# An expert loop whose down products move one tile later, between the next tile's up products

## The chip, the core and the metric

The kernel runs on one core of a Trainium2 chip. A core has five engines that run side by side and meet only through semaphores: TensorE (PE: matrix products into the PSUM banks), VectorE (DVE), ScalarE (ACT), GpSimd (POOL) and SyncE (SP: it starts transfers). The metric is the device time of one execution in microseconds. The kernel before takes 276.58 us, the median of three runs from 275.57 to 281.17.

## The reference

The input x holds 32 sequences of 64 tokens of 128 numbers (2048 tokens); the layer has two parts.

```python
x = x + xattn(layernorm(x), ctx)          # projections, FFT over the sequence, Hamilton products
x = x + ffn(layernorm(x))

def ffn(x):                               # 8 experts, top 2
    gate_logits = x @ gate_w + gate_b
    weights, indices = top_k(gate_logits, 2); weights = softmax(weights)
    h = einsum('bsd,edh->ebsh', x, w1) + b1            # 128 -> 1024 for each expert
    xh, gh = split(h, 2)
    act = silu(gh) * xh                                # 512
    out_e = einsum('ebsf,efd->ebsd', act, w2) + b2     # 512 -> 128
    return sum over the two chosen experts of out_e * weight
```

The change is in the second part. Each of the 2048 tokens picks two experts, so 4096 rows are computed.

## The kernel before

**Routing.** The kernel computes only the chosen experts. After the first part it ranks the 4096 (token, choice) pairs by expert and cuts them into tiles of 256 rows that never mix experts; with these inputs there are 21 tiles, and `MAX_TILES` is 23. A grid of matrix products (L1101) turns the ranks into lists: for each tile, from which rows of `xn_rows` (normalised tokens, in memory) its inputs come and to which rows of `y_rows` its outputs go. They lie in `lists_all`. The names `bounds` and `ends` are the numbers of the tile at which each expert ends, values that are known only at run time.

**The expert loop.** Every engine has eight loops in a row, one for each expert e, whose count comes from `ends`; all engines go over the same tiles t.

- POOL gathers the 256 rows of a tile with two indirect DMAs (two halves of 128, L900) into one of two slots of `xg`, and scatters a tile's results with two more (L918) from one of two slots of `y_sb`. The row numbers of both are first copied to `lists_now` (L910). [...] Its order per tile is: copy the lists, gather tile t+3, wait for y of tile t, scatter tile t.
- DVE copies the gathered rows to `x_now` (L786, `move_x`), which frees the slot.
- PE transposes them (L1109, `turn_x`) into bank 4; ACT rounds that to `xT_hi` (L455) and DVE keeps the rest as `xT_lo` (L781).
- PE makes the up products in four chunks c of 128 hidden units (banks 0 to 3), each of two parts with three matmuls: w1_hi by xT_hi (L1133), w1_hi by xT_lo (L1134) and w1_lo by xT_hi (L1135). The last matmul of a chunk signals `up_done`.
- ACT applies silu to the gate part (L466, `silu_ready`), DVE multiplies with the other part (L808, `act_ready`).
- PE makes the down products of chunk c from `act` and w2 (L1145, banks 5 and 6), sums over the four chunks and signals `down_done` once per tile. DVE adds b2 into `y_sb` (L816, `y_ready`); that write waits until the scatter that last read the slot has landed.

The order on PE for a tile is: up 0 to 3, transposes of tile t+1, down 0 to 3. The order on DVE is: act 0 to 3, xT_lo of t+1, y, move_x of t+2. The order is written out by hand, and each engine works strictly in its own order. DVE also makes `w1_lo` of experts 4 to 7 (L558) after the loops of experts 0 to 3.

**After the loop** SP waits until all scatters have landed, reads `y_rows` back (L339), ACT and DVE combine the two choices, and the output is written (L342).

## Time and profile before

| | us |
|---|---|
| median of three runs (lowest, highest) | 276.58 (275.57, 281.17) |
| the profiled execution's own time | 275.91 |
| its span, first to last instruction | 274.1 |
| first up matmul of the expert loop to the last scatter's issue, in the span | 115.65 to 255.62 |

The profile shows one execution. Times in its rows are in microseconds from the span's start, and a group's row gives how often an instruction ran, its busy time, the mean of one in ns, and how long its engine stood idle just before it and for whom. A line number is one of the code above. In the trace, a matmul of 32-bit data is shown as two instructions where both operands are full float32 (L1145, L1109), and as one for the rounded kind (L1133 to L1135). `prod` is the name of both `act` and `silu`, and `spec` the one of both `xg` and `y_sb`, since they share memory with tiles of the first part. "issue" means that no recorded event released the instruction, and "remote" that the releaser is not among the recorded instructions.

### The profile page before, as it was taken

To read this page: it belongs to the slowest core of one execution; us is meant where nothing else is said; L and a number is where in the kernel's file an instruction comes from. 1 tells how busy PE (TensorE), PEld (TensorE's weight loads), DVE (VectorE), ACT (ScalarE), POOL (GpSimd) and SP (SyncE) were. 2 spreads that over 40 slices of the span, in tenths; PEclk is the share of its full clock that TensorE was granted. 3 is DMA by queue.
4 is the path that set the end of the run, shared out by engine and by line. 5 is a ranking of instruction groups with operands and counts; after the bars stand their busy time and mean duration, and the time that the engine had idled before them with its cause. 6 is when DMAs were issued, how large, how long until landed. Compare 5 with 4: busy or idle time off the path is not lost.

```text
span 274.1 us, 4826 instructions
## 1 busy us (share of the span) xinstructions
PE 206.2 (75%) x1454; PEld 186.3 (68%) x1454; DVE 161.8 (59%) x435; ACT 89.5 (33%) x211; POOL 135.6 (49%) x201
## 2 busy tenths in 40 slices
PE   8999998999596018679796996979799739887000
PEld 5898777889586006469695985969799729787000
DVE  4783896999957898335353742445466234354145
ACT  0473541112184073033233523242333124233033
POOL 0100444455900070746675886868688873856300
PEclk9977999999777555999999999799999977999755
DMA  7999200000026500110211011111111112222095
GB/s 213 305 339 316 62 0 0 2 0 0 11 85 182 200 0 0 38 42 29 45 31 48 29 46 40 48 29 43 42 41 38 49 41 30 48 29 48 22 282 174
DMA packets 17918, 20.76 MB, mean 76 GB/s; under 512 B 2736, under 2 KB 13520, under 8 KB 17872
## 3 DMA queue, kind: packets, MB, share of 16 engines
q1 hardware_dynamic: 13520, 14.08, 16.8%
q0 software_dynamic: 3008, 5.87, 8.8%
q10 hardware_dynamic: 1376, 0.64, 1.0%
q8 instruction: 7, 0.11, 0.2%
q14 instruction: 7, 0.06, 0.1%
HBM read 15.63 MB, written 4.95 MB: 75 GB/s over the span
## 4 chain that ended last, share of the span: by engine, by line
PE 39%; DVE 17%; issue 12%; POOL 11%; another core or an unknown queue 8%; DMA 5%; ACT 4%; DVEq 2%; POOLq 1%; SPq 1%; ACTq 0%
PE bank L1145 7%; POOL y_rows L918 5%; PE bank L954 4%; POOL spec L900 4%; PE bank L1135 4%; PE bank L1006 3%; PE bank L1007 3%; PE bank L1133 3%; PE bank L969 3%; PE bank L1134 3%; DVE prod L577 2%; PE bank L991 2%; DVE shared_a L754 2%; DMA spec<-xn_rows,lists_now 2%
## 5 line engine op out<-in xcount | busy, mean ns | idle before, releaser
L466 ACT ACTIVATE prod<-bank,b_col 128x256 f32<-128x256 f32 x84 | 38.5, 474 | 93.2 <-PE bank L1135 65.0
L1145 PE MATMUL bank<-w_sb,prod 128*128 128x128 f32 x336 | 51.9, 299 | 18.3 <-DVE prod L808 11.8
L1145 PEld LDWEIGHTS bank<-w_sb,prod 128*128 128x128 f32 x336 | 44.1, 203 | 25.2 <-DVE prod L808 16.9
L808 DVE SCALAR_TENSOR_TENSOR prod<-bank,b_col,prod 128x256 f32<-128x256 f32 x84 | 37.8, 480 | 34.3 <-ACT prod L466 17.4
L1133 PE MATMUL bank<-xT_hi,w_hi 128*128 128x256 f32 x168 | 49.3, 294 | 0.2 <-DVE xT_lo L781 0.2
L918 POOL DMA_INDIRECT y_rows<-spec,lists_now x42 | 42.6, 1015 | 10.0 <-issue 8.7
L1134 PE MATMUL bank<-xT_lo,w_hi 128*128 128x256 f32 x168 | 47.3, 281 | 0.0
L1135 PE MATMUL bank<-xT_hi,w_lo 128*128 128x256 f32 x168 | 47.2, 281 | 0.0
L900 POOL DMA_INDIRECT spec<-xn_rows,lists_now x40 | 42.1, 1052 | 9.2 <-issue 9.0
L1133 PEld LDWEIGHTS bank<-xT_hi,w_hi 128*128 128x128 f32 x168 | 31.8, 189 | 0.8 <-issue 0.6
L1134 PEld LDWEIGHTS bank<-xT_lo,w_hi 128*128 128x128 f32 x168 | 31.8, 189 | 0.0
L1135 PEld LDWEIGHTS bank<-xT_hi,w_lo 128*128 128x128 f32 x168 | 31.7, 189 | 0.0
L816 DVE TENSOR_TENSOR spec<-bank,b_sb 128x256 f32 x21 | 8.9, 425 | 38.4 <-PE bank L1145 19.7
L861 POOL TENSOR_TENSOR half<-prod 128x512 f32<-128x512 f32 x7 | 9.0, 1280 | 33.0 <-DVE prod L577 33.0
L895 POOL TENSOR_TENSOR taken<-const 1x1 f32<-1x1 f32 x41 | 8.6, 210 | 24.0 <-DVE spec L816 21.5
L884 POOL TENSOR_TENSOR shared_b<-basis,choice_b 128x832 bf16<-128x832 bf16 x2 | 4.8, 2416 | 22.4 <-DVE basis L749 22.4
L1006 PE MATMUL bank<-basis,spec 128*128 128x256 f32 x48 | 15.4, 404 | 0.6 <-ACT spec L390 0.6
L1007 PE MATMUL bank<-basis,spec 128*128 128x256 f32 x48 | 15.2, 399 | 0.0
L1109 PE MATMUL bank<-const,x_now 128*128 128x128 f32 x44 | 8.6, 278 | 6.5 <-DVE x_now L786 4.7
L577 DVE TENSOR_TENSOR prod<-q_basis,bank 128x512 f32<-128x512 f32 x16 | 10.2, 680 | 5.5 <-ACT q_basis L397 5.5
L954 PE MATMUL bank<-warm 128*128 128x256 bf16 x81 | 12.1, 323 | 1.2 <-DVE warm L514 1.2
L397 ACT ACTIVATE q_basis<-bank 128x256 f32<-128x256 f32 x8 | 3.1, 384 | 29.5 <-PE bank L1007 29.5
(173 smaller groups left out, 360.0 us busy)
## 6 DMA issues: line engine op xcount, KB each, us to landing
xq<-in_L_ffn_w SPq DMA_DIRECT2D x2, 1024.0 KB, 6.3
xq<-y_rows SPq DMA_DIRECT2D x8, 256.0 KB, 4.9
xq<-in_x SPq DMA_DIRECT2D x2, 512.0 KB, 6.2
x_sb<-in_L_ffn_w SPq DMA_DIRECT2D x1, 1024.0 KB, 12.1
w_spare<-in_L_ffn_w SPq DMA_DIRECT2D x1, 1024.0 KB, 12.6
xn_rows<-xq SPq DMA_DIRECT2D x4, 256.0 KB, 2.4
out<-ctx_sb SPq DMA_DIRECT2D x4, 256.0 KB, 2.4
const<-const_table SPq DMA_DIRECT2D x1, 690.5 KB, 9.0
```

Of the source, the lines that this page charges most:

```text
L466: nc.scalar.activation(silu[:, c, :], bank[:, c, XT:2 * XT], ACT.Silu, bias=b1_col[:, e * 2 * FC + FC + c:e * 2 * FC + FC + c + 1]).then_i ...
L577: last = tt(o, l, r, ALU.mult)
L808: stt(act[:, c, :], bank[:, c, 0:XT], b1_col[:, e * 2 * FC + c:e * 2 * FC + c + 1], silu[:, c, :], ALU.add, ALU.mult).then_inc(act_ready, 1)
L900: nc.gpsimd.indirect_dma_start(out=xg[:, par, h, :], out_offset=None, in_=xn_dram, in_offset=bass.IndirectOffsetOnAxis(ap=offsets[:, h:h + ...
L918: nc.gpsimd.indirect_dma_start(out=y_dram, out_offset=bass.IndirectOffsetOnAxis(ap=lists_now[:, par, 1, h:h + 1], axis=0), in_=y_sb[:, par ...
L954: mm(bank[:, 0, 0:256], warm[:, 0:P], warm[:], start=True, stop=True)
L1006: mm(dst, src[:, 0], basis[:, i, 0, :], start=False, stop=False, skip_group_check=True)
L1007: last = mm(dst, src[:, 1], basis[:, i, 1, :], start=False, stop=True, skip_group_check=True)
L1133: mm(dst, w1_hi[:, e, cols], xT_hi[:], start=True, stop=False)
L1134: mm(dst, w1_hi[:, e, cols], xT_lo[:], start=False, stop=False)
L1135: last = mm(dst, w1_lo[:, e, cols], xT_hi[:], start=False, stop=True)
L1145: last = mm(bank[:, 5 + h, 0:D], act[:, c, h * P:(h + 1) * P], w2_sb[:, e * FC + c, :], start=(c == 0), stop=(c == FC - 1))
```

## The change

1. **Down products one tile later.** In step t, PE does up 0, up 1 of tile t; down 0, down 1 of tile t-1; the transposes of tile t+1; up 2, up 3 of tile t; down 2, down 3 of tile t-1. After the last loop come the down products of the last tile. Step 0 makes down products of a tile that doesn't exist, and nothing scatters their result. Since tile t-1 can be of another expert, PE works out which w2 to take (`of`) in registers, and DVE which b2.
2. **Two slots** for `xT_hi` and `xT_lo`, since the transposes now come in the middle of the up products that read the other slot.
3. **Signals.** `down_done` is given per chunk, and DVE's product of chunk c waits for it (`act` has one slot per chunk, so the old tile's down product must have read it). DVE's order is act 0, act 1, xT_lo, act 2, y of tile t-1, act 3, move_x, copy of the lists. ACT's order is silu 0, silu 1, xT_hi, silu 2, silu 3.
4. **POOL.** The copy of the lists moves to DVE. One wait, for `lists_taken`, begins a step of POOL; then come the scatter and the gather, in that order. Gathers run five tiles ahead of the scatter beside which they stand (three before), and five tiles are gathered ahead of the loop. Tiles past the last are no longer gathered.
5. The lists have room for 24 tiles rather than 26 (`NCOL` 48, not 52).

```diff
-AHEAD = 3
-NCOL = HALVES * (MAX_TILES + AHEAD)
+AHEAD = 5
+NCOL = HALVES * (MAX_TILES + 1)
...
-        xT_hi = sb("xT_hi", [P, XT], F32R)
-        xT_lo = sb("xT_lo", [P, XT], F32R)
+        xT_hi = sb("xT_hi", [P, 2, XT], F32R)
+        xT_lo = sb("xT_lo", [P, 2, XT], F32R)
...
@@ ScalarE, once per tile
-                    keep_xT_hi(t + 1)
+                        if c == 1:
+                            keep_xT_hi(t + 1)
...
@@ VectorE
+            def keep_act(t, e, c):
+
+                v.wait_ge(silu_ready, FC * t + c + 1)
+                v.wait_ge(down_done, FC * t + c + 1)
+                stt(act[:, c, :], bank[:, c, 0:XT], b1_col[:, e * 2 * FC + c:e * 2 * FC + c + 1],
+                    silu[:, c, :], ALU.add, ALU.mult).then_inc(act_ready, 1)
+
+            def keep_y(t, of):
+
+                v.wait_ge(down_done, FC * t + FC)
+                for h in range(HALVES):
+                    v.wait_ge(scattered[0][h], ((t + 1) // 2) * 16 + 16)
+                    v.wait_ge(scattered[1][h], (t // 2) * 16 + 16)
+                tt(y_sb[:, bass.ds((t + 1) % 2, 1)].rearrange("p o h d -> p (o h) d"), bank[:, 5:7, 0:D],
+                   b2_sb[:, bass.ds(of, 1), :].to_broadcast([P, HALVES, D]), ALU.add).then_inc(y_ready, 1)
+
+            def copy_lists(t):
+
+                cp(lists_now[:, bass.ds((t + 1) % 2, 1)].rearrange("p o k h -> p (o k h)"),
+                   lists_all[:, bass.ds(t + AHEAD - 1, 1)].rearrange("p o k h -> p (o k h)")).then_inc(lists_taken, 1)
...
-                    v.wait_ge(down_done, t + 1)
-                    for c in range(FC):
-                        v.wait_ge(silu_ready, FC * t + c + 1)
-                        stt(act[:, c, :], ...).then_inc(act_ready, 1)
+                    keep_act(t, e, 0)
+                    keep_act(t, e, 1)
                     keep_xT(t + 1)
-                    v.wait_ge(down_done, t + 2)
+                    keep_act(t, e, 2)
+                    keep_y(t, (t - start + MAX_TILES) // (MAX_TILES + 1) + (e - 1) if e else 0)
+                    keep_act(t, e, 3)
...
                     move_x(t + 2)
+                    v.wait_ge(y_ready, t + 2)
+                    v.wait_ge(x_moved, t + 3)
+                    copy_lists(t)
...
+            last = ends[E - 1]
+            keep_y(last, E - 1)
+            v.wait_ge(y_ready, last + 2)
+            copy_lists(last)
...
@@ GpSimd
-            def take_lists(t, par, pair):
-                ...
-            def scatter(t, par):
-                p.wait_ge(y_ready, t + 2)
-                take_waits(1)
+            def scatter(par):
...
+            def step(count, par, more=True):
+
+                p.wait_ge(lists_taken, count)
+                p.sem_inc(passed, 1)
+                scatter(par)
+                if more:
+                    gather(1 - par, lists_now[:, par, 0])
...
-            gather(0, lists_all[:, 2, 0])
-            with p.Fori(0, last // 2) as i:
+            for n in range(2, AHEAD):
+                p.wait_ge(x_moved, n - 1)
+                gather(n % 2, lists_all[:, n, 0])
+            pairs = last // 2
+            with p.Fori(0, pairs - 2) as i:
                 for par in range(2):
-                    t = 2 * i + par
-                    take_lists(t, par, i)
-                    take_waits(0)
-                    gather(1 - par, lists_now[:, par, 0])
-                    scatter(t, par)
+                    step(2 * i + par + 6, par)
+            for n in range(4):
+                step(2 * pairs + n + 2, n % 2, more=False)
...
@@ TensorE
+            def down(t, c, of):
+
+                pe.wait_ge(act_ready, FC * t + c + 1)
+                for h in range(HALVES):
+                    last = mm(bank[:, 5 + h, 0:D], act[:, c, h * P:(h + 1) * P],
+                              w2_sb[:, bass.ds(FC * of + c, 1), :].rearrange("p o d -> p (o d)"),
+                              start=(c == 0), stop=(c == FC - 1), skip_group_check=True)
+                last.then_inc(down_done, 1)
...
+                    pe.wait_ge(xT_ready, t + 1)
+                    up(0)
+                    up(1)
+                    pe.wait_ge(y_ready, t + 1)
+                    down(t, 0, of)
+                    down(t, 1, of)
                     pe.wait_ge(x_moved, t + 2)
                     turn_x()
-
-                    pe.wait_ge(y_ready, t + 1)
-                    for c in range(FC):
-                        pe.wait_ge(act_ready, FC * t + FC + c + 1)
-                        ...
-                    last.then_inc(down_done, 1)
+                    up(2)
+                    up(3)
+                    down(t, 2, of)
+                    down(t, 3, of)
+            last = ends[E - 1]
+            pe.wait_ge(y_ready, last + 1)
+            for c in range(FC):
+                down(last, c, E - 1)
```

How the instructions of a tile stand in the queues, as the program has them: after the line number come the operation, what it writes <- reads, the shape, and the semaphores that it waits for. "ISA" and "REGISTER_ALU" are register or semaphore instructions of the sequencer. The numbers of lines differ between the two kernels.

PE before, from the last up matmul of a tile to the first down product:

```order
L1135 MATMUL bank<-xT_hi,w_lo 128x256
L1138 REGISTER_ALU
L1109 MATMUL bank<-const,x_now 128x128 [waits x_moved]
L1109 MATMUL bank<-const,x_now 128x128
L1143 REGISTER_ALU [waits y_ready]
L1145 MATMUL bank<-w_sb,prod 128x128 [waits act_ready]
L1145 MATMUL bank<-w_sb,prod 128x128
```

PE now, from the last matmul of up 1 to the first of up 2 (L1149 are the down products of the tile before, L1130 the transposes, L1166 to L1168 the up products):

```order
L1168 MATMUL bank<-xT_hi,w_lo 128x256
L1149 ISA [waits act_ready,y_ready]
L1149 REGISTER_ALU
L1149 MATMUL bank<-w_sb,prod 128x128 x2
L1149 ISA [waits act_ready]
L1149 MATMUL bank<-w_sb,prod 128x128 x2
L1177 REGISTER_ALU
L1130 MATMUL bank<-const,x_now 128x128 [waits x_moved]
L1130 MATMUL bank<-const,x_now 128x128
L1161 REGISTER_ALU
L1166 MATMUL bank<-xT_hi,w_hi 128x256 [waits act_ready]
```

The waits for `act_ready` before the down products, which before followed on the same tile's up products, now regard the tile before; the wait for `y_ready` stands in the middle of the up products.

DVE before, from xT_lo to the end of the tile:

```order
L781 TENSOR_TENSOR xT_lo<-bank,xT_hi 128x256 [waits xT_hi_ready]
L814 ISA [waits down_done]
L815 ISA [waits scattered00]
L816 ISA [waits scattered11,scattered01,scattered10]
L816 TENSOR_TENSOR spec<-bank,b_sb 128x256
L819 REGISTER_ALU
L786 ISA [waits gathered01,gathered11,gathered10,gathered00]
L786 COPY x_now<-spec 128x256
```

DVE now, from y (L821) to the end of a step (L812 is act 3, L790 move_x, L826 the list copy):

```order
L821 TENSOR_TENSOR spec<-bank,b_sb 128x256
L812 SCALAR_TENSOR_TENSOR prod<-bank,b_col,prod 128x256 [waits down_done,silu_ready]
L841 ISA
L842 ISA [waits gathered00]
L790 ISA [waits gathered11,gathered01,gathered10]
L790 COPY x_now<-spec 128x256
L826 ISA [waits x_moved,y_ready]
L826 REGISTER_ALU
L826 COPY lists_now<-lists_all 128x4
```

The y of a tile now comes before the last of the four act products, and a wait for DVE's own x_moved and y_ready stands before the list copy.

POOL before, one tile:

```order
L909 ISA [waits x_moved]
L910 ISA [waits scattered01,scattered00]
L910 COPY lists_now<-lists_all 128x4
L912 REGISTER_ALU
L895 TENSOR_TENSOR taken<-const 1x1 [waits lists_taken]
L900 DMA spec<-xn_rows,lists_now 128x128 x2
L895 TENSOR_TENSOR taken<-const 1x1 [waits y_ready]
L918 DMA y_rows<-spec,lists_now 10752x128 x2
```

POOL now, one tile (L933 scatter, L926 gather):

```order
L933 DMA y_rows<-spec,lists_now 10240x128 [waits lists_taken]
L933 DMA y_rows<-spec,lists_now 10240x128
L926 DMA spec<-xn_rows,lists_now 128x128 x2
L939 REGISTER_ALU
```

The copy, both `taken` products and the waits for x_moved, y_ready and the scatters are gone from POOL; `lists_taken` stands for them all, and the scatter comes ahead of the gather.

## Rows read from the trace of the kernel before

**Rows 1.** The page: PE's busy time, and its granted clock in 40 slices.

```profile
PE 206.2 (75%) x1454; PEld 186.3 (68%) x1454; DVE 161.8 (59%) x435; ACT 89.5 (33%) x211; POOL 135.6 (49%) x201
PEclk9977999999777555999999999799999977999755
```

**Rows 2.** The page: the chain that ended last, shares by engine.

```profile
PE 39%; DVE 17%; issue 12%; POOL 11%; another core or an unknown queue 8%; DMA 5%; ACT 4%; DVEq 2%; POOLq 1%; SPq 1%; ACTq 0%
```

**Rows 3.** Stretches: length; PE, PEld, DVE, ACT, POOL busy (count); clock; DMA share, GB/s.

```profile
115.60:255.60 140.00, 115.90 (x882) 107.99 (x882) 64.66 (x152) 44.48 (x105) 96.84 (x144) 0.96 0.16 39
...
153.80:158.80 5.00, 5.00 (x45) 4.89 (x44) 3.75 (x8) 1.98 (x5) 4.32 (x5) 1.00 0.14 39
158.80:165.80 7.00, 5.75 (x46) 5.15 (x44) 2.99 (x7) 2.17 (x5) 5.72 (x9) 1.00 0.20 47
165.80:174.60 8.80, 6.79 (x44) 6.35 (x43) 2.71 (x7) 1.95 (x5) 5.68 (x10) 0.81 0.12 37
```

**Rows 4.** Groups by line, 115 to 255: busy us, mean ns | idle before, releasers.

```profile
L466 ACT ACTIVATE prod<-bank,b_col 128x256 f32<-128x256 f32 x84 | 38.5, 474 | 93.2 <-PE bank L1135 65.0 <-remote 21.5 <-issue 6.5
L808 DVE SCALAR_TENSOR_TENSOR prod<-bank,b_col,prod 128x256 f32<-128x256 f32 x84 | 37.8, 480 | 34.3 <-ACT prod L466 17.4 <-issue 16.7
...
L816 DVE TENSOR_TENSOR spec<-bank,b_sb 128x256 f32 x21 | 8.9, 425 | 38.4 <-PE bank L1145 19.7 <-remote 11.6 <-DMA y_rows<-spec,lists_now 5.1
L895 POOL TENSOR_TENSOR taken<-const 1x1 f32<-1x1 f32 x41 | 8.6, 210 | 24.0 <-DVE spec L816 21.5 <-issue 0.5
...
L786 DVE COPY x_now<-spec 128x256 f32 x21 | 6.3, 301 | 1.2 <-issue 0.8
...
L558 DVE TENSOR_TENSOR w_lo<-xq,w_hi 128x1024 fp32r<-128x1024 f32 x4 | 4.9, 1216 | 0.0
```

**Rows 5.** ACT in order of time: start, length, instruction [idle before <- releaser].

```profile
152.11 0.47 ACT L466 ACTIVATE prod<-bank,b_col 128x256 f32<-128x256 f32 x1 [0.24 <-PE bank L1135]
...
159.81 0.48 ACT L466 ACTIVATE prod<-bank,b_col 128x256 f32<-128x256 f32 x1 [2.11 <-PE bank L1135]
161.98 0.48 ACT L466 ACTIVATE prod<-bank,b_col 128x256 f32<-128x256 f32 x1 [1.70 <-PE bank L1135]
162.74 0.47 ACT L466 ACTIVATE prod<-bank,b_col 128x256 f32<-128x256 f32 x1 [0.28 <-PE bank L1135]
164.20 0.47 ACT L466 ACTIVATE prod<-bank,b_col 128x256 f32<-128x256 f32 x1 [0.99 <-remote]
...
169.36 1.57 ACT L466 ACTIVATE prod<-bank,b_col 128x256 f32<-128x256 f32 x4 [4.42 <-PE bank L1135]
```

**Rows 6.** PE in order of time: tiles' first matmul (L1133), chunks' last matmul (L1135).

```profile
115.65 0.38 PE L1133 MATMUL bank<-xT_hi,w_hi 128*128 128x256 f32 x1 [0.15 <-DVE xT_lo L781]
...
151.78 0.29 PE L1135 MATMUL bank<-xT_hi,w_lo 128*128 128x256 f32 x1
...
160.20 0.28 PE L1135 MATMUL bank<-xT_hi,w_lo 128*128 128x256 f32 x1
...
161.62 0.29 PE L1135 MATMUL bank<-xT_hi,w_lo 128*128 128x256 f32 x1
...
168.62 0.28 PE L1135 MATMUL bank<-xT_hi,w_lo 128*128 128x256 f32 x1
...
246.46 0.37 PE L1133 MATMUL bank<-xT_hi,w_hi 128*128 128x256 f32 x1
```

**Rows 7.** POOL in order of time.

```profile
160.05 0.20 POOL L910 COPY lists_now<-lists_all 128x4 int32 x1
...
161.99 0.96 POOL L900 DMA_INDIRECT spec<-xn_rows,lists_now  x1 [0.30 <-issue]
...
165.60 0.20 POOL L910 COPY lists_now<-lists_all 128x4 int32 x1
...
183.86 1.81 POOL L918 DMA_INDIRECT y_rows<-spec,lists_now  x1 [0.16 <-DVE x_now L786]
...
255.62 1.00 POOL L918 DMA_INDIRECT y_rows<-spec,lists_now  x1 [0.43 <-issue]
```

More of the change, by code:

```diff
@@ L801, in _ @@
             ends += [v.value_load(bounds[0:1, e:e + 1], min_val=e + 1, max_val=MAX_TILES) for e in range(E - 3, E)]
-            for e in range(E):
-                with v.Fori(ends[e - 1] if e else 0, ends[e]) as t:
-                    v.wait_ge(down_done, t + 1)
-                    for c in range(FC):
-                        v.wait_ge(silu_ready, FC * t + c + 1)
-                        stt(act[:, c, :], bank[:, c, 0:XT], b1_col[:, e * 2 * FC + c:e * 2 * FC + c + 1],
-                            silu[:, c, :], ALU.add, ALU.mult).then_inc(act_ready, 1)
+            def keep_act(t, e, c):
[3 more added lines that the diff above has]
+                    silu[:, c, :], ALU.add, ALU.mult).then_inc(act_ready, 1)
@@ L810, in _ @@
+            for e in range(E):
+                start = ends[e - 1] if e else 0
+                with v.Fori(start, ends[e]) as t:
+                    keep_act(t, e, 0)
+                    keep_act(t, e, 1)
                     keep_xT(t + 1)
-                    v.wait_ge(down_done, t + 2)
+                    keep_act(t, e, 2)
+                    keep_y(t, (t - start + MAX_TILES) // (MAX_TILES + 1) + (e - 1) if e else 0)
+                    keep_act(t, e, 3)
+                    here = t + 2 if e < E - 2 else t + 2 * ((ends[E - 1] // 2) * 2 >= t + 2)
@@ L813, in _ @@
                     for h in range(HALVES):
[L814 to L820 removed]
+                        v.wait_ge(gathered[0][h], (here // 2) * 16 + 16)
@@ L924, in _ @@
             gather(1, lists_all[:, 1, 0])
[L925 to L934 removed]
+            for n in range(2, AHEAD):
[3 more added lines that the diff above has]
+            with p.Fori(0, pairs - 2) as i:
+                for par in range(2):
+                    step(2 * i + par + 6, par)
+            for n in range(4):
+                step(2 * pairs + n + 2, n % 2, more=False)
             with p.If(last % 2 == 1):
[L937 to L938 removed]
+                step(2 * pairs + 6, 0, more=False)
         @block.tensor
@@ L1122, in _, with up @@
             pe.wait_ge(w2_in, 16)
+            def down(t, c, of):
[5 more added lines that the diff above has]
+                last.then_inc(down_done, 1)
             for e in range(E):
                 pe.wait_ge(w1_ready, e + 1)
-                with pe.Fori(ends[e - 1] if e else 0, ends[e]) as t:
-                    pe.wait_ge(xT_ready, t + 1)
-                    for c in range(FC):
+                start = ends[e - 1] if e else 0
+                with pe.Fori(start, ends[e]) as t:
+                    of = (t - start + MAX_TILES) // (MAX_TILES + 1) + (e - 1) if e else 0
+                    def up(c):
                         pe.wait_ge(act_ready, FC * t + c + 1)
```

54 lines of the change are left out of this document (19 added, 35 removed).

## The prediction, made before the changed kernel ran

> **What bounds the kernel now.** I read the page, then the stretches of the expert loop, then ACT, PE and POOL in order of time. PE is busy for three quarters of the span and leads the chain that ended last with 39%, but "issue", DVE, POOL and unnamed releasers share most of the rest [rows 1, 2]: no engine alone sets the loop. The loop's 140.0 us hold 115.9 of PE, 96.8 of POOL, 64.7 of DVE [rows 3]. From the first to the twenty-first tile's first matmul it is 130.81 us, 6.54 a tile [rows 6]. The tiles are unequal. Of those 20 periods, 8 last 4.86 to 5.37 us, 9 last 6.01 to 7.73, 3 last 8.28, 8.82 and 12.03. In a short one PE is busy all the time, with the same 45 or so matmuls [rows 3]; so PE's own work is about 4.95 us a tile, 104 for 21, and some 33 us of the loop are waiting.
>
> What the long tiles wait for is the point. Where all goes well, ACT starts silu 0.33 us after the chunk's last matmul started (151.78 to 152.11) [rows 5, 6]. In the tile from 158.80, chunk 1's last matmul starts at 160.20, but ACT starts at 161.98, 1.45 late by that offset; chunk 3's at 161.62, and ACT at 164.20, 2.25 late. In the next tile the last of 24 up matmuls starts at 168.62, and ACT sits idle for 4.42 us and then finds all four chunks at 169.36. DVE is not what ACT waits for. I read this as **PE's completion signals reaching others late**, by 0 to 3 us, and that hurts since down c waits for act c, which waits for silu c, which waits for the signal. The long tiles lie mostly where POOL has issued indirect DMAs for several us without a pause (nothing but work from 160.05 to 165.60 [rows 7]); the short ones lie after a pause of it. That is a correlation of this trace, not a cause shown.
>
> POOL is the next bound. With nothing to wait for, its round took 5.55 us, from list copy to list copy (160.05 to 165.60), with 1.0 us per indirect DMA and 0.30 between two [rows 7].
>
> **Part by part.**
>
> *Down products one tile later.* What PE waits for after up 3 (silu, act: 0.47 and 0.48 us [rows 4]) is now a tile old. PE's work a step stays at 4.95. I lay out a step from its first up matmul: up 0 and 1 to 1.42 (12 matmuls in 1.42 us, 160.20 to 161.62 [rows 6]); down 0 and 1 to 2.35; transposes to 2.6; up 2, 3 to 4.0; down 2, 3 to 4.95. With the 0.33 for a signal: act 0 runs at 2.2, act 1 by 3.2, xT_lo by 3.7 (needed at 4.95), act 2 from 4.8, y from 5.3 to 5.9, act 3 to 6.4, move_x to 6.8 (0.30 each [rows 4]), the list copy to 7.1. In the next step PE wants y before down 0, at 4.95 + 1.42 = 6.37 or a little after, and move_x before the transposes, at 7.5. So act has over 2 us to spare, move_x 0.7, and **y only 0.5 to 0.8**: y is what is late next. DVE has 4 x 0.48 + 2 x 0.43 (y, and xT_lo taken as long) + 0.30 + 0.2 = 3.3 us of work in a step and stays off the bound. The w1_lo pieces (1.22 us, four times [rows 4]) come after the list copy and delay act 0 to 8.4, where 10 would do: nothing.
>
> *Extra work.* One more set of down products, 16 x 0.118 = 1.9 us, stands at the loop's end, while the first tile's useless set stands in step 0. PE's registers for `of` run in the sequencer; those after a wait that comes late are bare. No row shows them; between 0 and 0.3 us a step I take 0.1, near the former end, since the short tiles show no gap for the registers that are there now.
>
> *POOL.* The list copy (0.20 [rows 7]) and two `taken` (0.21 each [rows 4]) go, with gaps: 5.55 becomes 4 x (1.0 + 0.30) = 5.2, with the wait and the signal of a step 5.25. So a step is **5.25** at best, PE's 5.05 hidden under it; in the last five steps, without gathers, the two are reversed, and I keep 5.25. Where DVE makes w1_lo, one DMA took 1.81 for 1.0 [rows 7]; that is as before, four times 0.8, and the scatter has some 3.5 us to spare. The Trainium skill ("SBUF — State Buffer", the part on shared ports) has DVE's copies in the fast modes hold off GpSimd, while it infers that a tensor_tensor leaves descriptor writing alone; the row of 1.81 beside L558, a tensor_tensor, speaks against the inference. By that page the new list copy and move_x could hold POOL too, up to 0.5 us a step, which would make 10 us of the whole where POOL binds; my sum has nothing for it.
>
> *Three more signals per tile from PE.* The four up signals of a tile on time come 0.71 apart, at no visible cost: zero. The Trainium skill ("TensorE: Matmul & The Clock Gate", The cost: per-tile semaphore tail) prices each increment at 26 ns; 63 more would be an estimated 1.7 us if all lay on the path.
>
> *Gathers earlier, smaller lists.* A gather still has two steps to land, as before. The lists' grids shrink by 4 of 52 columns ahead of the loop: a small gain, of a part that these rows don't show, left out. Loop start stays at 115.65.
>
> *Late signals.* They stay; the change only makes more room. A signal 1.45 late makes y late by 1.45 - 0.75 = 0.7: such a step takes 5.95. A signal 2.25 or more late finds PE stalled at y after 12 matmuls, and the one case in the rows where PE ran dry (168.62) had its signals 0.4 after that; so the stall is about 0.95, the step 6.2. With the mix of before (8 on time, 10 late with the last, 3 very late): 8 x 5.25 + 10 x 5.95 + 3 x 6.2 = 120.1 us, 5.72 a step.
>
> **The sum.** The last step ends at 115.65 + 120.1 = 235.75. Then come the last down products 1.9, signal 0.3, y and list copy 0.8, POOL's start 0.4: the last scatter is issued at 239.2, where now it is at 255.62 [rows 7]. What follows is unchanged. So 16.4 us less than 275.91, the profiled execution, is 259.5; the median stands 0.67 above that execution: **260 us**.
>
> **The rivals.**
>
> *A. The signals come on time* because PE never stands still before them, or the room covers them. For it: short tiles are those where nothing waits. 21 x 5.25 = 110.25; the last scatter at 229.3; 26.3 less: 250. Chance 0.28 (247 to 253).
>
> *B. The forecast*, 254 to 267: 0.42.
>
> *C. Lateness grows with POOL's load.* POOL's pauses, after which signals were on time, vanish when POOL is the bound. Say 12 steps at 5.95, and 9 with signals 2.5 us late that no stall flushes, 5.25 + 2.5 - 0.75 = 7.0: 134.4 us, last scatter at 253.5, **274**. For it: the correlation above. Against it: a stalled PE gives POOL its pauses back. Chance 0.18 (268 to 281). A fall of PE's clock belongs here: it was at the lower of its levels (1.2 GHz) in part of the 8.80 us tile, mean 0.81, after PE stood idle for 2 us [rows 3, 6].
>
> *D. Slower: the loop through y.* Down 3 of step t signals, DVE adds y, PE waits for y in the midst of the next up products, with everything behind it, and DVE's act 3, move_x and POOL's lists queue behind the same y. If that signal is 2.5 us late every time, each step is 7.0: 147 us, last scatter at 266.05, **287**. It decides from a mean step of (139.97 - 3.4) / 21 = 6.50 us, a mean lateness of 2.0. Against it: half of the tiles before had less. Chance 0.12.
>
> *The change doesn't do what it says*: not likely, since the queues show the order. If POOL's DMAs took 1.3 us, it would look like C.
>
> **The numbers.** 2% (5.5 us) is about what a measurement of this kernel can tell. Faster by over 2% is below 271: A, B and 0.04 of C, 0.74. Within 2%: the rest of C, 0.14. Slower: D, 0.12. The range from 247 to 275 holds A, B and over half of C.
>
> **What would show it.** Step periods from PE's first up matmul of a tile: 5.2 to 5.3 (A), about 5.7 with a mix (B), 6.4 (C), 7 (D). PE's idle time should stand before the down products, released by y, and no longer by act. ACT's idle time before silu no longer matters, though silu would still start late. POOL's round should be 5.2 to 5.3 with little idle time. The last scatter is issued near 239. I am wrong if PE idles before up products or transposes for long, if POOL's round without a wait is above 5.5, or if the signals are late by an amount that goes with the number of waits rather than with POOL.

## The result, and the profile after

The changed kernel took **300.24 us** (median of 4 runs, 299.47 to 303.75); the kernel before, on the same chip, 277.76 (275.57 to 281.17). The ratio is 1.088, 95% interval 1.080 to 1.096: slower, where 260 was forecast. The profiled execution took 300.84, its span is 299.0. Medians here and below are over all executions; ratios leave out those in which a kernel ran slower than its fastest by more than 1.5%.

From the page of the changed kernel: PE's busy time and clock, the chain, then groups by line (busy us, mean ns | idle before, releaser).

```profile
PE 218.5 (73%) x1470; PEld 200.9 (67%) x1470; DVE 165.2 (55%) x458; ACT 91.3 (31%) x211; POOL 116.7 (39%) x138
...
PEclk9957999999665559899789879969979889599855
...
PE 48%; DVE 16%; another core or an unknown queue 13%; issue 8%; DMA 6%; ACT 3%; DVEq 3%; POOL 1%; POOLq 1%; SPq 0%; ACTq 0%
...
L1166 PE MATMUL bank<-xT_hi,w_hi 128*128 x168 | 55.8, 332 | 24.6 <-DVE xT_lo L785 24.6
L933 POOL DMA_INDIRECT y_rows<-spec,lists_now x42 | 42.6, 1014 | 71.9 <-DVE lists_now L826 62.5
L1149 PE MATMUL bank<-w_sb,prod 128*128 (+1 forms) x352 | 53.8, 298 | 11.1 <-DVE spec L821 6.1
```

POOL left the chain (11% in [rows 2], 1% now) and stands idle for 62.5 us, waiting for the list copy of a step. PE loses 24.6 us before the up products, behind xT_lo, and only 6.1 before the down products, behind y. "Another core or an unknown queue" grew from 8% to 13%: one core runs here, so these are releasers that the profile can't name.

The loop, from PE's first up product to the issue of the last scatter, with the columns of [rows 3]:

```profile
116.87:281.92 165.05, 125.74 (x898) 120.41 (x898) 68.33 (x175) 46.38 (x105) 77.73 (x79) 0.89 0.12 32
```

Before, it was 139.97 us with 115.90 of PE at a mean clock of 0.96. Of the 25.1 us more, 15.2 are idle time of PE (24.1 before, 39.3 now) and 9.8 are busy time; the extra set of down products is some 1.9 of the latter, and the rest are the same matmuls at a lower mean clock.

The same stretch in three views. First ACT in order of time (start, length, instruction, idle before), where L467 is silu and L455 keeps xT_hi:

```profile
157.24 0.38 ACT L455 ACTIVATE xT_hi<-bank 128x256 f32 x1 [1.10 <-PE bank L1130]
157.82 0.48 ACT L467 ACTIVATE prod<-bank,b_col 128x256 f32<-128x256 f32 x1 [0.20 <-PE bank L1168]
...
161.13 0.47 ACT L467 ACTIVATE prod<-bank,b_col 128x256 f32<-128x256 f32 x1 [2.12 <-PE bank L1168]
166.12 0.47 ACT L467 ACTIVATE prod<-bank,b_col 128x256 f32<-128x256 f32 x1 [4.51 <-remote]
169.13 0.38 ACT L455 ACTIVATE xT_hi<-bank 128x256 f32 x1 [2.54 <-remote]
169.41 0.83 ACT L467 ACTIVATE prod<-bank,b_col 128x256 f32<-128x256 f32 x2
```

PE, with L1130 the transposes, L1149 the down products and L1168 a chunk's last up product:

```profile
156.68 0.38 PE L1130 MATMUL bank<-const,x_now 128*128 128x128 f32 x2
...
160.55 0.28 PE L1168 MATMUL bank<-xT_hi,w_lo 128*128 x1
...
161.88 0.38 PE L1130 MATMUL bank<-const,x_now 128*128 128x128 f32 x2
...
165.40 0.36 PE L1149 MATMUL bank<-w_sb,prod 128*128 x1 [0.44 <-issue]
170.45 0.58 PE L1166 MATMUL bank<-xT_hi,w_hi 128*128 x1 [4.68 <-DVE xT_lo L785]
170.82 0.41 PE L1167 MATMUL bank<-xT_lo,w_hi 128*128 x1
171.04 0.41 PE L1168 MATMUL bank<-xT_hi,w_lo 128*128 x1
```

And POOL, within a stretch without a pause that began at 157.54:

```profile
160.14 0.99 POOL L926 DMA_INDIRECT spec<-xn_rows,lists_now  x1 [0.30 <-issue]
161.43 0.96 POOL L926 DMA_INDIRECT spec<-xn_rows,lists_now  x1 [0.30 <-issue]
162.70 1.15 POOL L933 DMA_INDIRECT y_rows<-spec,lists_now  x1 [0.30 <-issue]
...
165.45 0.99 POOL L926 DMA_INDIRECT spec<-xn_rows,lists_now  x1 [0.30 <-issue]
166.74 0.96 POOL L926 DMA_INDIRECT spec<-xn_rows,lists_now  x1 [0.30 <-issue]
```

The transposes at 156.68 are answered by ACT 0.56 later. Those at 161.88 are answered at 169.13, 7.25 later: 6.7 us late. ACT takes its signals in order, and stood idle for 4.51 us before chunk 1's silu and for another 2.54 before these. Chunk 1's signal (160.55) is answered at 166.12; by the 0.33 us of [rows 5, 6] that is 5.2 late. PE meanwhile runs until 165.76 and then stands for 4.68. The last signals arrive together, 1.4 us after POOL's last indirect DMA ended at 167.70. After that stall PE's matmuls lie 0.21 us apart and not 0.12: the granted clock is 0.50 of full speed, the lower level of 1.2 GHz, as the stretches show (columns as in [rows 3]):

```profile
161.80:165.80 4.00, 3.19 (x25) 2.66 (x23) 1.18 (x1) 0.00 (x0) 3.09 (x4) 1.00 0.20 59
165.80:170.40 4.60, 0.00 (x0) 0.00 (x0) 1.63 (x4) 1.59 (x4) 1.60 (x2) 0.88 0.20 34
170.40:173.40 3.00, 2.95 (x14) 2.96 (x15) 1.34 (x5) 0.48 (x1) 0.30 (x1) 0.50 0.00 0
```

POOL's indirect DMAs in the loop now come in stretches without a pause (no gap between two DMAs over 0.45 us) of 10.0 to 10.3 us, five times, and of about 5 us between them. Before, the list copy and the tiny products `taken` stood in each round and made one gap of 0.62 us; by the same measure the longest stretch of that loop was 6.0.

The kernel before had such late signals too, in its 12.03 us tile (PE's last matmul of chunks 0 and 3, ACT's silu and DVE's product of the same chunks):

```profile
217.22 0.28 PE L1135 MATMUL bank<-xT_hi,w_lo 128*128 128x256 f32 x1
...
219.35 0.27 PE L1135 MATMUL bank<-xT_hi,w_lo 128*128 128x256 f32 x1
...
222.20 0.47 ACT L466 ACTIVATE prod<-bank,b_col 128x256 f32<-128x256 f32 x1 [6.51 <-remote]
222.70 0.48 DVE L808 SCALAR_TENSOR_TENSOR prod<-bank,b_col,prod 128x256 f32<-128x256 f32 x1 [1.36 <-issue]
...
226.63 0.47 ACT L466 ACTIVATE prod<-bank,b_col 128x256 f32<-128x256 f32 x1 [1.01 <-remote]
227.14 0.48 DVE L808 SCALAR_TENSOR_TENSOR prod<-bank,b_col,prod 128x256 f32<-128x256 f32 x1 [1.00 <-issue]
```

By the offset of 0.33 us these silus start 4.65 and 6.95 us late. POOL had then worked since 196.56 with no gap of over 0.96 us between two of its DMAs. So gaps of 0.62 us don't keep signals on time in a long run of rounds. What differs is how often: a silu starts over 4 us late 4 times in one tile before, and 15 times in six tiles now; the mean over all 84 is 1.1 us before and 1.3 now. Signals between the others pass at once beside the same scatters: ACT ends chunk 0's silu at 222.67 and DVE starts at 222.70; DVE ends at 223.18 and PE starts at 223.24.

The lateness and the stretches go together in time; whether the one makes the other is what the experiments ask. They ran on chips 1, 3, 5 and 6, each seen at one time only; the number of the first result's chip isn't on record. **The kernel before took 257.6 and 257.4 us on two of them (chips 1 and 6), 279.6 and 281.3 on the others (3 and 5)**; the first result is of the latter sort. Whether the sort is a lasting property of a chip, or of the time at which it was used, no run shows; "chip" below means both. Each comparison is within a chip.

### The profile page after: what moved, and what is told of

The parts are those of the page before. It is cut to its first block, busy times and chain, and to the rows that moved or that the text cites. A ratio compares the mean times of both kernels' runs of the same rounds, so it can differ in the third digit from the quotient of the medians.

```text
span 299.0 us, 5025 instructions
## 1 busy us (share of the span) xinstructions
PE 218.5 (73%) x1470; PEld 200.9 (67%) x1470; DVE 165.2 (55%) x458; ACT 91.3 (31%) x211; POOL 116.7 (39%) x138
## 4 chain that ended last, share of the span: by engine, by line
PE 48%; DVE 16%; another core or an unknown queue 13%; issue 8%; DMA 6%; ACT 3%; DVEq 3%; POOL 1%; POOLq 1%; SPq 0%; ACTq 0%
PE bank L1149 10%; PE bank L1166 6%; PE bank L1168 5%; PE bank L1167 5%; PE bank L975 4%; DMA y_rows<-spec,lists_now 3%; PE bank L1027 3%; PE bank L1028 3%; PE bank L990 3%; DVE shared_a L756 2%; PE bank L1012 2%; DVE prod L579 2%; DMA xq<-y_rows 2%; ACT xq L437 2%
## 5 line engine op out<-in xcount | busy, mean ns | idle before, releaser
L812 DVE SCALAR_TENSOR_TENSOR prod<-bank,b_col,prod 128x256 f32<-128x256 f32 x84 | 39.3, 480 | 67.3 <-remote 31.2
L1166 PE MATMUL bank<-xT_hi,w_hi 128*128 x168 | 55.8, 332 | 24.6 <-DVE xT_lo L785 24.6
L933 POOL DMA_INDIRECT y_rows<-spec,lists_now x42 | 42.6, 1014 | 71.9 <-DVE lists_now L826 62.5
L1149 PE MATMUL bank<-w_sb,prod 128*128 (+1 forms) x352 | 53.8, 298 | 11.1 <-DVE spec L821 6.1
L467 ACT ACTIVATE prod<-bank,b_col 128x256 f32<-128x256 f32 x84 | 38.8, 474 | 72.4 <-PE bank L1168 50.3
L1149 PEld LDWEIGHTS bank<-w_sb,prod 128*128 128x128 f32 x352 | 48.1, 210 | 14.9 <-issue 14.5
L1166 PEld LDWEIGHTS bank<-xT_hi,w_hi 128*128 128x128 f32 x168 | 36.0, 214 | 26.3 <-issue 26.3
L1167 PE MATMUL bank<-xT_lo,w_hi 128*128 x168 | 51.2, 305 | 0.0
L1168 PE MATMUL bank<-xT_hi,w_lo 128*128 x168 | 51.1, 304 | 0.0
L1167 PEld LDWEIGHTS bank<-xT_lo,w_hi 128*128 128x128 f32 x168 | 36.3, 216 | 0.0
L1168 PEld LDWEIGHTS bank<-xT_hi,w_lo 128*128 128x128 f32 x168 | 35.7, 213 | 0.0
L926 POOL DMA_INDIRECT spec<-xn_rows,lists_now x32 | 31.3, 977 | 9.7 <-issue 9.7
L455 ACT ACTIVATE xT_hi<-bank 128x256 f32 (+1 forms) x22 | 8.5, 384 | 48.9 <-PE bank L1130 26.1
L821 DVE TENSOR_TENSOR spec<-bank,b_sb 128x256 f32 x22 | 9.3, 425 | 12.3 <-DMA y_rows<-spec,lists_now 6.4
L926 POOL DMA_INDIRECT spec<-xn_rows,lists_all x10 | 9.9, 994 | 13.9 <-issue 9.4
L579 DVE TENSOR_TENSOR prod<-q_basis,bank 128x512 f32<-128x512 f32 x16 | 10.2, 680 | 6.5 <-ACT q_basis L397 6.5
L785 DVE TENSOR_TENSOR xT_lo<-bank,xT_hi 128x256 f32 (+1 forms) x22 | 9.3, 423 | 7.4 <-ACT xT_hi L455 4.5
L915 POOL TENSOR_TENSOR shared_b<-basis,choice_b 128x768 bf16<-128x768 bf16 x2 | 4.5, 2276 | 21.9 <-DVE basis L751 21.9
```

The lines of the kernel that those rows point to most:

```text
L467: nc.scalar.activation(silu[:, c, :], bank[:, c, XT:2 * XT], ACT.Silu, bias=b1_col[:, e * 2 * FC + FC + c:e * 2 * FC + FC + c + 1]).then_i ...
L579: last = tt(o, l, r, ALU.mult)
L812: stt(act[:, c, :], bank[:, c, 0:XT], b1_col[:, e * 2 * FC + c:e * 2 * FC + c + 1], silu[:, c, :], ALU.add, ALU.mult).then_inc(act_ready, 1)
L926: nc.gpsimd.indirect_dma_start(out=xg[:, par, h, :], out_offset=None, in_=xn_dram, in_offset=bass.IndirectOffsetOnAxis(ap=offsets[:, h:h + ...
L933: nc.gpsimd.indirect_dma_start(out=y_dram, out_offset=bass.IndirectOffsetOnAxis(ap=lists_now[:, par, 1, h:h + 1], axis=0), in_=y_sb[:, par ...
L1149: last = mm(bank[:, 5 + h, 0:D], act[:, c, h * P:(h + 1) * P], w2_sb[:, bass.ds(FC * of + c, 1), :].rearrange("p o d -> p (o d)"), start=( ...
```

## Experiments

**1. No indirect DMAs in the loop** (chip 1). The loops compute on rows loaded once; nothing is gathered or scattered, the waits for it are gone, and the end reads x in place of `y_rows`. The cut in the changed kernel, and the same in the one before:

```diff
             def scatter(par):
-                for h in range(HALVES):
-                    nc.gpsimd.indirect_dma_start(
...
+                pass
...
                 if more:
-                    gather(1 - par, lists_now[:, par, 0])
+                    pass
```

> The changed kernel, without the indirect DMAs of the expert loop: POOL keeps its waits for the lists but neither gathers nor scatters (only the first two tiles are gathered, their rows serve all tiles, and the end reads x in place of y_rows). Theory P (POOL's indirect DMAs, issued for some 4 us and more without a pause, hold up PE's completion signals): signals on time, step 5.0 to 5.3 us, time 245 to 255. Rival Q (any DMA traffic does it): the same here. Rival R (PE's own order does it, by its many signals and the waits in its sequencer): signals late as before, step over 6.5, time above 285. Rival Y (the loop through y as I forecast it, needing no DMA): steps of 7, PE waiting for y.

> The kernel before, in the same way without the indirect DMAs of the loop (the list copy and the small products of POOL stay; the first two tiles' rows serve all tiles, and the end reads x in place of y_rows). Theory P and rival Q: all 21 tiles last 4.9 to 5.1 us, time 237 to 245. Rival R: the long tiles of 6 to 12 us stay, time 270 or more.

Measured: 240.3 us (237.9 to 244.6) for the changed kernel so cut, 236.8 (235.2 to 238.9) for the one before, beside 257.6 uncut. Both lie below what I had expected (245 to 255, and 237 to 245), the second by a hair. Every signal is on time and the tiles are 4.87 and 4.85 us long. So without POOL's DMAs **the new order on PE gains nothing**: the old one already runs at PE's own pace, and PE waits 0.1 us in all before its down products. This chip shows no late signals uncut either, so it can't tell what holds them up.

**2. Plain DMAs from SP in place of the indirect ones** (chips 1, 6 and 5). Rows are moved by position and not by the lists.

```diff
+            def step(count, par, at, more=True):
+                sp.wait_ge(lists_taken, count)
+                for h in range(HALVES):
+                    sp.dma_start(y_dram[bass.ds(at + P * h, P)], y_sb[:, par, h, :]).then_inc(scattered[par][h], 16)
+                if more:
+                    gather(1 - par, par)
```

> The changed kernel with the gathers and scatters as plain DMAs of the same size (128 rows of 512 bytes) from SP's queue in place of POOL's indirect ones (rows in order rather than by list: what is gathered and where it goes is not what the lists say). Same waits, same bytes, same number of DMAs. Theory P: as without DMAs, 245 to 257. Rival Q (traffic, or the DMAs' own semaphore writes): as the changed kernel, 290 or more. Rival R: 285 or more.

> The changed kernel with its loop's row gathers and scatters as plain DMAs of the same size, issued by SP: rows are moved by position and not by the lists, so its output is another. It took 246.9 us on the chip where the kernel before took 257.6. Theory: POOL's indirect DMAs are all that makes one chip slower than the other, so on any chip it takes 246 to 249, 50 us less than the changed kernel where that takes 300. Rival, that the chip is slower for another reason (clock, memory): 265 or more there.

> The changed kernel with SP's plain DMAs in place of POOL's indirect ones, rows by position. Theory: 246 to 250 on any chip, also where the kernel before takes 278. Rival (the chip is slower for another reason): 265 or more there.

Measured: 246.9 us, 248.8 and 247.7 (245.8 to 248.9). All three are in the ranges expected. The last is on chip 5, where the kernel before took 281.3: ratio 0.878 (0.871 to 0.885). **With the same bytes and no indirect DMAs the two sorts of chip are alike.**

**3. A probe behind the kernel before** (chips 1 and 3): five stages, in each 24 groups of six matmuls on PE, every group signalled to a small ACT instruction. POOL does nothing, 12 gathers, 12 scatters, 12 additions of 128x512; in the fifth SP issues 12 plain DMAs.

```diff
+                for n in range(GROUPS):
+                    for i in range(6):
+                        last = mm(bank[:, n % 4, 0:XT], w1_hi[:, 0, 0:P], xT_hi[:], start=True, stop=True)
+                    last.then_inc(m_up, 1)
```

> The kernel before, with five stages after its end, in each of which PE makes 24 groups of 6 matmuls (256 columns, rounded float32), each group's last with a signal for which ACT waits, some 17 us. Beside it: stage 0 nothing; stage 1 POOL issues 12 gathers; stage 2 POOL issues 12 scatters; stage 3 POOL does 12 additions of 128x512; stage 4 SP issues 12 plain DMAs of the size of the gathers. Theory P: ACT's rows 0.71 us apart in stages 0, 3 and 4, and in stages 1 and 2 late from about the fourth indirect DMA on, by up to several us. Rival Q: late in 1, 2 and 4. Rival R: on time in all.

> The probe once more (the kernel before, then five stages: nothing; 12 gathers by POOL; 12 scatters; 12 additions; 12 plain DMAs by SP), on the chip of this call. Where before takes 257: all signals 0.71 us apart again. Where it takes 277: theory P expects late signals in stages 1 and 2 alone; rival Q in 4 too; a theory of PE by itself in all five.

On chip 1 ACT's instructions stand 0.71 us apart in all stages, but for the first few of a stage. There my theory, which expected late signals beside the DMAs, missed. On chip 3 they are 0.71 apart in the first, fourth and fifth. The stage with the gathers there, ACT:

```profile
301.31 0.21 ACT L491 ACTIVATE m_out<-b_col 128x16 f32<-128x16 f32 x1 [0.50 <-issue]
302.01 0.21 ACT L491 ACTIVATE m_out<-b_col 128x16 f32<-128x16 f32 x1 [0.49 <-PE bank L1190]
303.29 0.21 ACT L491 ACTIVATE m_out<-b_col 128x16 f32<-128x16 f32 x1 [1.07 <-PE bank L1190]
304.75 0.22 ACT L491 ACTIVATE m_out<-b_col 128x16 f32<-128x16 f32 x1 [1.24 <-PE bank L1190]
306.87 0.21 ACT L491 ACTIVATE m_out<-b_col 128x16 f32<-128x16 f32 x1 [1.90 <-PE bank L1190]
309.72 0.21 ACT L491 ACTIVATE m_out<-b_col 128x16 f32<-128x16 f32 x1 [2.64 <-remote]
314.61 0.74 ACT L491 ACTIVATE m_out<-b_col 128x16 f32<-128x16 f32 x6 [4.67 <-PE bank L1190]
```

PE, which here waits for nobody within a stage:

```profile
297.45 10.67 PE L1190 MATMUL bank<-xT_hi,w_hi 128*128 128x256 f32 x88 [0.35 <-SPq L348]
308.99 0.28 PE L1190 MATMUL bank<-xT_hi,w_hi 128*128 128x256 f32 x1 [0.87 <-issue]
...
311.79 0.50 PE L1190 MATMUL bank<-xT_hi,w_hi 128*128 128x256 f32 x2 [1.12 <-issue]
...
314.59 8.32 PE L1190 MATMUL bank<-xT_hi,w_hi 128*128 128x256 f32 x48 [0.33 <-issue]
```

And POOL's first and last gather of it:

```profile
297.67 0.98 POOL L961 DMA_INDIRECT xq<-xn_rows,lists_all  x1 [36.04 <-SPq L348]
...
311.48 0.94 POOL L961 DMA_INDIRECT xq<-xn_rows,lists_all  x1 [0.30 <-issue]
```

For 4.3 us signals are on time; then they fall further and further behind while PE keeps its pace. From 308.1 on PE itself goes in bits, with no wait in its program; that it can't run further ahead of its signals is my reading, not shown. Six signals come at once at 314.6, 2.2 us after the last gather. The scatters do the same (on time to 4.3 us into them, then up to 4.2 us between two). Each chip was probed once, and each stage has its control in the same execution. The effect is POOL's indirect DMAs on PE's signals; neither additions on POOL nor plain DMAs make it. This is **cause shown, on this chip**.

**4. The changed kernel on other chips** (3 and 6).

> The changed kernel itself, on the chip of this call beside the kernel before. Where the kernel before takes some 257 us, as in the last comparison, its signals are on time there (the probe's are), and theory P, with lateness only at some places or times, expects the changed kernel at my case A: 245 to 252, faster than before. Where before takes some 277, I expect 300 again, and signals up to 7 us late. A theory in which the new order itself costs 8% expects the ratio 1.09 in either place.

> The changed kernel once more, beside the kernel before on the same chip. The kernel before took 257.6 us on one chip and 279.6 on another. Held-up signals (my theory): on a chip where the kernel before takes about 258, signals come on time under the changed kernel too, its step is POOL's round of 5.2 to 5.3 us, and it takes about 248 to 252; on a chip where it takes about 280, 300 again. Rival, that the new order is slow in itself: slower by 8% on either chip.

Chip 3: 300.5 us against 279.6, ratio 1.080 (1.071 to 1.089), as at first. Chip 6: **252.4 (251.5 to 254.8) against 257.4, ratio 0.982 (0.974 to 0.989)**. That is faster beyond the interval, by just under the 2% that I had called measurable, and 0.4 us above the 248 to 252 expected; the rival's 8% slower isn't seen. There POOL issues indirect DMAs for 86.3 us without a pause and no signal is late. POOL and PE in that profile:

```profile
156.75 1.00 POOL L933 DMA_INDIRECT y_rows<-spec,lists_now  x1 [0.31 <-issue]
...
161.89 1.00 POOL L933 DMA_INDIRECT y_rows<-spec,lists_now  x1 [0.30 <-issue]
...
167.04 1.00 POOL L933 DMA_INDIRECT y_rows<-spec,lists_now  x1 [0.30 <-issue]
...
172.46 1.00 POOL L933 DMA_INDIRECT y_rows<-spec,lists_now  x1 [0.30 <-issue]
```

```profile
L1166 PE MATMUL bank<-xT_hi,w_hi 128*128 x168 | 50.9, 303 | 0.5 <-DVE xT_lo L785 0.3
L1149 PE MATMUL bank<-w_sb,prod 128*128 (+1 forms) x352 | 47.6, 278 | 2.9 <-DVE spec L821 1.4
```

POOL's round is 5.15 us, or 5.42 where one DMA took 1.24; from the sixth to the twentieth y the step is 5.26 (147.69 to 221.35, 14 steps). Of PE's waits in the loop, 24.6 us become 0.5 and 11.1 become 2.9.

**5. Only POOL's part of the change** (chip 3): PE's, ACT's and DVE's order as before; POOL's step as in the change, four tiles ahead, with the list copy on DVE.

```diff
+                    v.wait_ge(y_ready, t + 2)
+                    v.wait_ge(x_moved, t + 3)
+                    cp(lists_now[:, bass.ds(t % 2, 1)].rearrange("p o k h -> p (o k h)"),
...
-                    take_lists(t, par, i)
-                    take_waits(0)
-                    gather(1 - par, lists_now[:, par, 0])
-                    scatter(t, par)
...
+                    step(2 * i + par + 1, par)
```

> Only POOL's part of the change, on the kernel before: list copy by DVE, one wait per step, scatter then gather, gathers four tiles ahead; PE, ACT and x slots as before. If POOL's round (5.55 us before) binds where signals are on time: 4 to 7 us less than before. If late signals bind: DMAs follow each other more closely, so no gain or a few us more than before.

Measured 299.9 us (295.2 to 302.4) against 279.6 (277.2 to 284.2) before and 300.5 for the whole change; the two fastest of its four executions took 295.2 and 298.9. I had expected "a few us more" at most. POOL's part alone brings nearly the whole loss, some 16 to 20 us of 21, with stretches of 10 us as in the change. It holds three things at once: the copy and the `taken` gone from POOL, one wait for all four DMAs of a round, and gathers further ahead. Which of them does it isn't shown. The wait then stands before the down products:

```profile
L1137 PE MATMUL bank<-w_sb,prod 128*128 128x128 f32 x336 | 53.9, 311 | 32.2 <-DVE prod L810 21.3 <-issue 10.8
```

**6. Half as many signals of the down products** (chip 3).

```diff
-                last.then_inc(down_done, 1)
+                if c % 2 == 1:
+                    last.then_inc(down_done, 1)
```

> The changed kernel with two down signals a tile (after chunks 1 and 3) in place of four: 7 signals of PE a step, 9 with the change, 6 before. Where signals are late: if each signal takes a fixed time to get out (0.7 or 1.4 us, the steps seen in the trace), this saves 1 to 3 us a step, 275 to 290 for 300; if lateness is a matter of POOL's stretch alone, 296 to 304. Where signals are on time: within 2 us of the changed kernel.

DVE waits for the pair's signal where it waited for a chunk's. Measured 300.6 us (297.7 to 304.6), ratio to before 1.075 (1.066 to 1.083), beside 300.5 for the change with all of them. The number of down signals isn't it.

**7. A pause put into POOL's round.** An addition, and a tiny one that waits for it, between scatters and gathers. Once with 128x512, once with 128x192, each on chip 6 and on chip 5.

```diff
                 scatter(par)
                 if more:
+                    tt(pause_out[:], x1_sb[:, 0:4, :].rearrange("p a b -> p (a b)"),
+                       x1_sb[:, 4:8, :].rearrange("p a b -> p (a b)"), ALU.add).then_inc(paused, 1)
+                    p.wait_ge(paused, count - 5)
+                    tt(pause_one[:], C("pcol", 1), C("pcol", 1), ALU.add)
                     gather(1 - par, lists_now[:, par, 0])
```

> The changed kernel, with an addition of 128x512 and one of 1x1 that waits for it on POOL between a round's scatters and its gathers, in the 17 or so rounds that gather: POOL's round grows from 5.17 to about 6.7 us (1.36 us for such an addition in the probe). It adds 25 us of work to the engine whose round was the shortest possible step. Theory (signals are held up only in a stretch of indirect DMAs without a pause, and come free about 1.2 us into a pause): signals on time or nearly, steps at POOL's 6.7 instead of 7.3, 18 x 0.6 = 11 us faster than the changed kernel on a chip where that takes 300: 287 to 292. On a chip where nothing is held up: slower than the changed kernel by 18 x 1.4 = 25 us. Rival one, the number of indirect DMAs counts and not their pauses, or an addition on POOL is no pause: signals late as before, 300 to 310. Rival two, the signals wait for POOL's queue itself to be empty: no change from 300.

> The same with the addition cut to 128x192, about 0.6 us by its share of the 1.36: POOL's round about 5.9. Theory: since signals came free 1.2 to 1.5 us after POOL's stretches ended, 0.6 us is too short a pause to free them all: between the changed kernel and the one with the longer pause, 290 to 302; if any pause frees them, steps of 5.9 and 275 to 280. On a chip where nothing is held up: slower than the changed kernel by 18 x 0.7 = 13 us.

> The kernel with the 128x512 addition between scatters and gathers again; on the chip where nothing is held up it took 276.3 against 252.4 of the changed kernel (24 us for 17 pauses of 1.4). If the kernel before takes about 278 here, so that signals are held up: theory (only stretches without a pause hold them up), 280 to 292, faster than the changed kernel's 300 although POOL has 24 us more to do; rival (the number of DMAs counts, or an addition is no pause), 300 to 324. If the kernel before takes about 258: 276 again.

> The same with 128x192; 264.9 on the chip where nothing is held up. If the kernel before takes about 278: theory, some of the signals come free in 0.6 us of pause, 285 to 302; rival, 300 to 313. If the kernel before takes about 258: 265 again.

| | chip 6 | chip 5 |
|---|---|---|
| before | 257.4 | 281.3 |
| changed | 252.4 | not run |
| with 128x512 | 276.3 (274.0 to 279.0) | 281.1 (280.2 to 282.9), ratio 1.001 (0.997 to 1.005) |
| with 128x192 | 264.9 (264.5 to 265.4) | 282.9 (280.4 to 284.5), ratio 1.006 (1.002 to 1.011) |

On chip 6 the 16 pauses cost about what they last: 23.9 and 12.5 us, against 25 and 13 expected. On chip 5 both kernels are level with the one before; the changed kernel, 8 to 9% above it on both chips of this sort where it ran, would stand at 304 or more by that ratio. **So 24 us more work on POOL makes the kernel over 20 us faster there.** The rivals gave 300 or more. The comparison with the changed kernel goes through that ratio, as it didn't run on chip 5. All of these kernels issue the same 84 indirect DMAs, so their number isn't it.

POOL on chip 5, with the short pause:

```profile
154.61 0.60 POOL L946 TENSOR_TENSOR pause_out<-x_sb 128x192 f32<-128x192 f32 x1
155.28 0.18 POOL L949 TENSOR_TENSOR pause_one<-const 1x1 f32<-1x1 f32 x1
155.62 0.99 POOL L929 DMA_INDIRECT spec<-xn_rows,lists_now  x1 [0.15 <-issue]
156.91 0.96 POOL L929 DMA_INDIRECT spec<-xn_rows,lists_now  x1 [0.30 <-issue]
158.18 1.23 POOL L936 DMA_INDIRECT y_rows<-spec,lists_now  x1 [0.31 <-issue]
...
160.71 0.62 POOL L946 TENSOR_TENSOR pause_out<-x_sb 128x192 f32<-128x192 f32 x1
```

No stretch of the loop is longer than 5.1 us in this profile; the eight gathers ahead of it last 10.2. I had put 285 to 302 on the short pause and missed it: the kernel with gaps of 1.0 us takes as long as the one with 1.7. Lateness isn't gone: a silu starts up to 2.7 us late with the longer pause and 4.5 with the short one, and the short one's 282.9 is 18 us above its time on chip 6, where the longer one's is 5. So a shorter round is paid back in late signals, and the two sizes end level. No version here that moves the right rows beats the kernel before on both sorts of chip.

## Why the prediction was wrong

**The step that failed is "Late signals".** I took the mix of before over, "They stay; the change only makes more room", with lateness of 0 to 3 us, and came to 5.72 us a step. The changed kernel's loop, from PE's first up product at 116.87 to the last scatter at 281.92, is 165.05 us; I had 123.55 (115.65 to 239.2). These 41.5 us are the whole error: with 1.2 more before the loop and 1.4 less behind it, 259.5 becomes 300.8. From the first to the twentieth y a step took 7.69 us (123.94 to 270.13, 19 steps).

The term was too small even for the kernel before. I read lateness of 0 to 3 us, took 168.62 for the one case where PE ran dry, and so put 6.2 us on each of the three very late steps. One of those three was the tile of 12.03 us, with signals up to 6.95 us late and PE dry from 219.6 on; I had its length in my list and didn't ask for its cause.

On this sort of chip lateness isn't a fixed amount for which an order on PE can make room. It grows with the length of POOL's stretches, as the probe shows, and I had shortened nothing but the pauses in them. The two `taken` and the list copy, which I priced at 5.55 less 5.25 us a round as pure gain, made the gap of 0.62 us in each round, and before them the scatters had a wait of their own. Without both, two rounds run on for 10 us, and signals are over 4 us late in six tiles where it was one. Experiments 5 and 7 show that POOL's part does it and that pauses undo it; that it was these small instructions and not the joint wait is argued. The 12.03 us tile, which came after 20 us of rounds with gaps of 0.62 us, shows that such a gap isn't enough by itself.

**Rival C named the mechanism and had the size wrong.** It had 9 steps with signals 2.5 us late, 274. Its counter-argument, "a stalled PE gives POOL its pauses back", is what is seen in POOL's stretches of 10 us and waits of about 5, but that is the slow cycle itself, no rescue. It also costs clock: C had mentioned it, and after the stall of 4.68 us PE ran at 1.2 GHz. The mean up product of line 1168 took 304 ns, beside 281 in the kernel before, with and without indirect DMAs. That is the busy time above, some 8 of the loop's 25 us; my sum had nothing for it.

**Rival D had the sign and not the place.** It gave 287 by a loop through y, which costs PE 6.1 us. The longer way was xT: turned rows signalled to ACT, xT_hi, its signal to DVE, xT_lo, needed 2.6 us after the transposes' start by my own layout (4.95 less 2.35). I had checked DVE's part of that chain with the signal on time and listed only y as what is late next. By the layout it has 1.25 us to spare (xT_lo by 3.7, needed at 4.95), more than y; but it has PE's signal at its start, where 6.7 us late leaves some 5 us of stall (4.68 in the rows). I gave it no price. PE idle before up products stood among my signs of being wrong, and came true with 24.6 us.

**What held.** Where signals are on time, rival A was right: 250 forecast, 252.4 on chip 6, with steps of 5.26 for 5.25 and POOL's round of 5.15 for 5.2. DVE's list copy and `of` cost nothing that shows. The Trainium skill ("SBUF — State Buffer", Who interferes with whom) has DVE's copies in the 2-port modes hold off GpSimd, which writes the descriptors of its DMAs. On chip 6 the indirect DMAs into which DVE's two copies a step fell took 0.94 to 1.10 us, as others do, so these runs bear out leaving that out; in which mode the copies ran no run shows. The four that took 1.19 to 1.43 stand beside DVE's `w1_lo`, a tensor_tensor, as does the 1.81 of [rows 7].

But the gain is small. PE's new order, the heart of the change, is worth nothing without indirect DMAs (4.87 for 4.85 us a tile, experiment 1), and nothing on the other sort of chip (experiment 5 takes no longer without it). The 5.0 us on chip 6 are then likely POOL's shorter round, an estimate of 21 x 0.3 = 6. The probe's profile on chip 1 agrees: it begins with the kernel before, every signal is on time, and its 20 tile periods are 110.4 us or 5.52 each, near POOL's round of 5.55. POOL's part alone wasn't run on such a chip.

**The correlation was in my rows and I used it in one direction.** I wrote that long tiles lie where POOL had issued for several us without a pause, and then took pauses away and kept the lateness.

## What to carry to other kernels

Where a correlation in the profile ties a delay to an engine's load, the sum must let that delay change with the load; "stays as it is" is itself a forecast and needs a row. Removing small instructions from a queue can remove the gaps that something else lives on; test with a deliberate pause, which adds work and so tells the gaps apart from the amount of work. Ask of the longest case in a list of periods what it waited for before averaging it with others. And when a chain is given room, price each wait of it with the late signal, not only the one that looks tightest.

## What was not expected of the hardware

On chips of one sort, PE's completion signals fall behind from some 4.3 us into a stretch of POOL's indirect DMAs 0.3 us apart, by up to 6.7 us, and the last come free 1.4 to 2.2 us after its end. In the kernel before, with gaps of 0.62 to 0.96 us, one tile's were up to 6.95 us late and came one by one while POOL was still at work. A gap of 1.0 us within each round of four kept the changed kernel level with the one before. Signals from ACT to DVE and from DVE to PE passed within 0.1 us beside the same DMAs. On chips of the other sort 86 us of such DMAs hold up nothing. Gathers and scatters do it, plain DMAs of the same size from SP and additions on POOL don't. The same kernel before so takes 257 or 280 us, and the same change is 1.8% faster or 8 to 9% slower: **a verdict on one chip needn't hold on another.** What differs between the chips, or between the times at which they were used, stays open. So does where signals and these DMAs meet, and whether it is the signal or the end of the matmul that is held up, since the ends of matmuls in the profile are modelled.
